# The key products of the two 16-head attentions moved to the end of a batch, three batches ahead

## The chip, the cores and the metric
The program runs on one core of one Trainium2 chip. The metric is the device time of one execution in microseconds (us); before the change the median of three runs is 4884.3 us (4883.45 to 4888.38).

## The reference, cut to what matters
The program is four layers of cross-attention and feed-forward over x (32 batches of 56 rows of 128) and a context (32 batches of 1500 rows of 128). The change touches the attention of layers L1 and L2, which have 16 heads of 8 columns:

```python
qh = split(q @ Wq.T + bq)          # (32, 16, 56, 8)
kh = split(k @ Wk.T + bk)          # (32, 16, 1500, 8), k is the context
vh = split(v @ Wv.T + bv)          # v is the context too
scores = jnp.einsum('bhqd,bhkd->bhqk', qh, kh) / jnp.sqrt(jnp.float32(D_K))
scores = jnp.where(mask[:, None, None, :] == 0, jnp.float32(-1000000000.0), scores)
attn = jax.nn.softmax(scores, axis=-1)
out = jnp.einsum('bhqk,bhkd->bhqd', attn, vh)
```

L1 has the mask and the biases, L2 has neither. Everything is float32.

## The kernel before, in words
`attention_16_heads` (L697) is called once for L1 and once for L2. All five instruction streams are unrolled over B = 32 batches. For one batch b they do the following.

- **Keys.** TensorE makes the keys of a batch as two items, ("keys", b, 0) with two products of 128x500 and ("keys", b, 1) with one (`keys_product`, L1020). VectorE empties them into the one tile `k_full` (L1189 with the mask of `valid` in L1, L1193 in L2), ScalarE copies them rounded into `k_hi` (L1131), GpSimd makes the remainder `k_lo` (L984). There is one `k_full`, one `k_hi` and one `k_lo`.
- **Moves.** SyncE (SP in the rows) issues 12 DMAs per batch in `move_keys` (L937 for `k_hi`, eight; L941 for `k_lo`, four), which lay the keys out by group of four heads in one of NKB = 3 tiles `keys`, on 96 partitions, so that one product carries high and low parts. In L1 two mask rows (L932) go with them. A tile is free when all scores of three batches earlier are made.
- **Rows.** Twelve items ("rows", b, n), n = 0 to 11, are the scores with the query on the partitions (`score_rows`, L1042); VectorE reduces them to maxima (L1202, L1205), and after n = 11 to one column `max_col` (L1211). ("turn", b, 0) transposes the column on TensorE (L1051), VectorE splits it (L1220, L1222), and SP moves it into two rows of the query tile (`move_maxima`, L949). The rows of batch b + 1 are made during batch b.
- **Scores and values.** In KT = 12 steps t, `scores(b, t, 0)` and `scores(b, t, 1)` (L1079) make a tile each, ScalarE takes the exponential (L1169) into `probs`, and `values(b, t)` (L1094, 16 small products) adds probabilities times values; the values are called in threes: 0 to 2 in step 4, 3 to 5 in step 7, 6 to 8 in step 10, and 9 to 11 at the start of the next batch. ScalarE then takes the sums (`take_acc`, L1154).

The order around the change is written out by hand, in lists that all engines follow in order. `before_scores` are the items at the start of a batch, `step_items[t]` those of step t; ("keys", 2, 0) in a list means the keys of two batches ahead. TensorE makes the first two items of `before_scores`, then values 9 to 11 of the batch before, then the other two, then the steps; in a step the first item comes between the two scores and the rest after them and after the values. The items share two pairs of PSUM banks in turn, so an item waits until the one two places before it is emptied. ScalarE goes through the same lists: after the two exponentials of a step it takes the keys or values of that step, and only then the next exponential. `prologue` is the order ahead of batch 0.

The first rows item of a batch (L1042, n = 0) waits for the queries, for all moves of that batch's keys, and in L1 for the mask rows. SP goes through one list too: in the turn for batch b it loads the context of b + 3 (`load_context`, L909, which waits for the last values product of b + 1, made in step 3 of batch b, because `ctx_T` has two tiles), then moves the keys of b + 2, then loads the mask row `valid` (L915) and the query terms (`load_terms`, L921) of b + 3, then moves the maxima of b + 1. GpSimd goes through the batches with `spread_queries(b)` (L994) ahead of `take_keys_lo(b, ·)`.

Of the kernel before, what the change touches and what calls it, by code (L numbers as in the profile page):

```python
# [20 lines left out]
B, SQ, D = 32, 56, 128  # L21
# [33 lines left out]
def bcast(ap, n, at):  # L55

    shape = list(ap.shape)
    return ap.unsqueeze(at).broadcast_to(shape[:at] + [n] + shape[at:])
# [638 lines left out]
def attention_16_heads(nc, s, a, layer, masked, biased):  # L697
# [14 lines left out]
    ROWS = PAIRS + SINGLES  # L712
# [1 line left out]

    before_scores = [("rows", 1, 0), ("keys", 2, 0), ("keys", 2, 1), ("rows", 1, 1)]
    step_items = [[("rows", 1, n)] for n in range(2, ROWS)] + [[], []]
    step_items[1].append(("values", 1, 0))
    step_items[3].append(("values", 1, 1))  # L720
    step_items[5].append(("sums", -1, 0))
    step_items[11].append(("turn", 1, 0))


    def of_batch(b, items):
        return [(kind, b + ahead, n) for kind, ahead, n in items if 0 <= b + ahead < B]

    prologue = [("keys", b, n) for b in range(2) for n in range(2)] + [("values", 0, n) for n in range(2)]
    prologue += [("rows", 0, n) for n in range(ROWS)] + [("turn", 0, 0)]
    scratch = list(prologue)  # L730
    for b in range(B):
        scratch += of_batch(b, before_scores)
# [29 lines left out]
    def key_cols(n):  # L762
        return slice(0, 2 * KC) if n == 0 else slice(2 * KC, SK)

    with ExitStack() as ctx:
        def sb(name, shape, dt=F32, on=ctx):
            return on.enter_context(nc.sbuf_tensor(f"{layer}a_{name}", shape, dt))
# [113 lines left out]
        keys = [sb(f"keys{n}", [KS, G, SK], F32R) for n in range(NKB)]  # L881
# [22 lines left out]
        @block.sync  # L904
        def _(sp):
            def load_context(b):
                if b >= 2:
                    sp.wait_ge(products, made[("values", b - 2, 1)])
                sp.dma_start(ctx_T[b % 2][:, :, :], a["ctx_T"][b].rearrange("d (t p) -> d t p", t=KT))\  # L909
                    .then_inc(ctx_loaded[b % 2], 16)  # L910

            def load_valid(b):
                if b:
                    sp.wait_ge(scratch_dve, by_dve[("keys", b - 1, 1)])
                sp.dma_start(valid[:, 0:SK], valid_dram[b:b + 1].broadcast_to([D, SK])).then_inc(valid_loaded, 16)  # L915

            def load_terms(b):
                if b >= 2:
                    sp.wait_ge(queries_made, (b - 1) * G)
                for k in range(3):  # L920
                    sp.dma_start(q_terms[b % 2][k * GR:(k + 1) * GR, :, :],  # L921
                                 q_dram[k, :, b * SQ:(b + 1) * SQ].rearrange("(g r) q -> r g q", g=G))\
                        .then_inc(terms_loaded[b % 2], 16)

            def move_keys(b):

                if b >= NKB:
                    sp.wait_ge(scores_made, (b - NKB + 1) * KT * 2)
                if b == 0:
                    sp.wait_ge(ones_set, NKB + NQ)  # L930
                if masked:
                    sp.dma_start(keys[b % NKB][KQ:KQ + 2, :, :].bitcast(F32), bcast(neg_dram[b], G, 1))\  # L932
                        .then_inc(neg_moved[b % NKB], 16)
                sp.wait_ge(k_hi_made, b * 2 + 2)
                for g in range(G):
                    for k in (0, 2):
                        sp.dma_start(keys[b % NKB][k * GR:(k + 1) * GR, g, :].bitcast(F32),  # L937
                                     k_hi[g * GR:(g + 1) * GR, :].bitcast(F32)).then_inc(keys_moved, 16)
                sp.wait_ge(k_lo_made, b * 2 + 2)
                for g in range(G):  # L940
                    sp.dma_start(keys[b % NKB][GR:2 * GR, g, :].bitcast(F32),  # L941
                                 k_lo[g * GR:(g + 1) * GR, :].bitcast(F32)).then_inc(keys_moved, 16)

            def move_maxima(b):
                sp.wait_ge(scratch_dve, by_dve[("turn", b, 0)])
                if b >= NQ:
                    sp.wait_ge(scores_made, (b - NQ + 1) * KT * 2)
                for k, part in enumerate((max_hi, max_lo)):
                    sp.dma_start(queries[b % NQ][SHIFT + k:SHIFT + k + 1, :, :].bitcast(F32), part[:, b % 2, :].bitcast(F32))\  # L949
                        .then_inc(row_moved, 16)  # L950

            if masked:
                load_valid(0)
            load_context(0)
            load_terms(0)
            load_terms(1)
            load_context(1)
            move_keys(0)
            if masked:
                load_valid(1)  # L960
            move_keys(1)
            if masked:
                load_valid(2)
            load_terms(2)
            load_context(2)
            move_maxima(0)
            for b in range(B):
                if b + 3 < B:
                    load_context(b + 3)
                if b + 2 < B:  # L970
                    move_keys(b + 2)
                if b + 3 < B:
                    if masked:
                        load_valid(b + 3)
                    load_terms(b + 3)
                if b + 1 < B:
                    move_maxima(b + 1)

        @block.gpsimd
        def _(pool):  # L980
            def take_keys_lo(b, n):
                cols = key_cols(n)
                pool.wait_ge(k_hi_made, b * 2 + n + 1)
                nc.gpsimd.tensor_tensor(k_lo[:, cols], k_full[:, cols], k_hi[:, cols].bitcast(F32), ALU.subtract)\  # L984
                    .then_inc(k_lo_made, 1)
                pool.wait_ge(k_lo_made, b * 2 + n + 1)

            def spread_queries(b):

                pool.wait_ge(terms_loaded[b % 2], 48 * (b // 2) + 48)  # L990
                if b >= NQ:
                    pool.wait_ge(scores_made, (b - NQ + 1) * KT * 2)
                for g in range(G):
                    nc.gpsimd.tensor_tensor(queries[b % NQ][0:KQ, g, :].rearrange("p (h q) -> p h q", h=HPG),  # L994
                                            bcast(q_terms[b % 2][:, g, :], HPG, 1),
                                            bcast(group_mask[0:KQ, :], SQ, 2), ALU.mult).then_inc(queries_made, 1)
                pool.wait_ge(queries_made, b * G + G)

            for n in range(NKB):
                nc.gpsimd.memset(keys[n][KQ:KS, :, :].bitcast(F32), 1.0).then_inc(ones_set, 1)  # L1000
            for n in range(NQ):
                nc.gpsimd.memset(queries[n][KQ:KS, :, :].bitcast(F32), 1.0).then_inc(ones_set, 1)
            pool.wait_ge(ones_set, NKB + NQ)
            for u in range(2):
                nc.gpsimd.memset(v[u][:, :, :, DK:DK + 1], 1.0).then_inc(ones_set, 1)
            pool.wait_ge(ones_set, NKB + NQ + 2)
            for b in range(B):
                spread_queries(b)
                for n in range(2):
                    take_keys_lo(b, n)  # L1010

        @block.tensor
        def _(pe):
# [46 lines left out]
            def make(item):  # L1060
                if item[0] == "keys":
                    keys_product(item)
                elif item[0] == "values":
                    values_product(item)
                elif item[0] == "rows":
                    score_rows(item)
                elif item[0] == "turn":
                    turn(item)
                else:
                    spread_sums(item)  # L1070
# [28 lines left out]
            for item in prologue:  # L1099
                make(item)  # L1100
            for b in range(B):
                for item in of_batch(b, before_scores[:2]):
                    make(item)
                if b:
                    for n in range(KT - GT, KT):
                        values(b - 1, n)
                for item in of_batch(b, before_scores[2:]):
                    make(item)
                for t in range(KT):
                    scores(b, t, 0)  # L1110
                    for item in of_batch(b, step_items[t][:1]):
                        make(item)
                    scores(b, t, 1)
                    if t > GT and (t - 1) % GT == 0:
                        for n in range(t - 1 - GT, t - 1):
                            values(b, n)
                    for item in of_batch(b, step_items[t][1:]):
                        make(item)
# [1135 lines left out]
```

## Time and profile before

| | us |
|---|---|
| runs, median of 3 | 4884.3 |
| profiled execution | 4889.31 |
| its span, first to last instruction | 4887.5 |
| first rows item of batch 2 to that of batch 30 ahead, L1 (28 periods) | 883.0 |
| the same in L2 (28 periods) | 860.7 |

The span is shared among the engines as PE 82%, DVE 55%, ACT 40%, POOL 20%. PE is TensorE (PEld its weight loads), DVE VectorE, ACT ScalarE, POOL GpSimd, SPq the queue from which SyncE issues DMAs. The attention of L1 fills the span from about 517 to 1582 us, that of L2 from about 1908 to 2945 us. PEclk in the windows is the granted clock of TensorE as a share of 2.4 GHz; 0.50 is 1.2 GHz. A row of the timeline gives start, duration, engine, source line, output and input, the count of instructions merged, and in brackets the idle time of the engine ahead of it and what ended it; "issue" says that the profile shows nothing that the engine waited for.

### The profile page before, as it was taken

The page shows a single profiled execution, that of the slowest core. Times are in us where ns is not written, and L with a number is a line of the kernel's source. Part 1 is how long each engine was busy: PE and PEld are TensorE (multiplying, and loading weights), DVE is VectorE, ACT ScalarE, POOL GpSimd, SP SyncE. Part 2 cuts the span into 40 slices and gives each one's busy share as a digit, 9 for nine tenths or more (in the row PEclk, how much of TensorE's full clock was granted, in tenths as well). Part 3 has the DMA queues.
Part 4 walks back from the last instruction along what each step waited for, and adds up shares of the span by engine and source line. Part 5 has one row for each costly group of instructions (what it writes and reads, how often), then busy time and mean ns, then how long its engine had stood idle before and what let it go on. Part 6 is the DMA issues. An engine that isn't in the chain of part 4 may idle for free. (4 is left out here: it accounts for less than half of the span.)

```text
span 4887.5 us, 95999 instructions
## 1 busy us (share of the span) xinstructions
PE 4009.1 (82%) x39918; PEld 2475.7 (51%) x39918; DVE 2668.6 (55%) x3910; ACT 1968.9 (40%) x3760; POOL 994.9 (20%) x979
## 2 busy tenths in 40 slices
PE   7799588888888896888888884358988988898888
PEld 4544366666666543566666662223444444444444
DVE  3233355555654332566656653337777777777751
ACT  3200144444444000344444452114555555555542
POOL 0000211111111002211111112102333343333330
PEclk8899699999999798899999997669999999999988
DMA  8700355555543001444444430000000000000000
GB/s 234 214 0 0 111 131 133 133 125 129 134 125 71 35 0 48 115 106 106 106 106 106 106 73 5 12 25 13 13 20 20 20 13 20 19 18 15 13 1 21
DMA packets 107980, 329.11 MB, mean 67 GB/s; under 512 B 54151, under 2 KB 55247, under 8 KB 107023
## 3 DMA queue, kind: packets, MB, share of 16 engines
q1 hardware_dynamic: 107567, 323.20, 25.4%
q8 instruction: 308, 5.05, 0.5%
q14 instruction: 105, 0.86, 0.1%
HBM read 168.20 MB, written 7.00 MB: 36 GB/s over the span
## 5 line engine op out<-in xcount | busy, mean ns | idle before, releaser
L1705 POOL TENSOR_TENSOR l_S<-l_S,l_shift 125x448 f32<-125x448 f32 (+1 forms) x416 | 459.3, 1138 | 311.2 <-ACT l_shift L1931 306.3
L1169 ACT ACTIVATE L2a_probs<-ps 125x448 f32<-125x448 f32 x768 | 375.0, 545 | 187.0 <-PE ps L1079 177.0
L1169 ACT ACTIVATE L1a_probs<-ps 125x448 f32<-125x448 f32 x768 | 374.9, 546 | 169.3 <-PE ps L1079 159.4
L1202 DVE TENSOR_REDUCE L1a_chunk_max<-ps 112x1 f32<-112x1000 f32 x256 | 300.5, 1196 | 249.2 <-PE ps L1042 248.7
L1759 PE MATMUL ps<-l_wk,l_xnT 128*125 128x512 f32 (+1 forms) x832 | 426.8, 639 | 2.3 <-ACT l_k_squares L1912 1.7
L1202 DVE TENSOR_REDUCE L2a_chunk_max<-ps 112x1 f32<-112x1000 f32 x256 | 300.6, 1196 | 218.1 <-PE ps L1042 217.7
L1777 PE MATMUL ps<-l_G,l_xnT 128*125 128x448 f32 (+1 forms) x832 | 388.8, 549 | 32.1 <-DVE l_S L2028 32.1
L1912 ACT ACTIVATE l_k_squares<-ps 125x512 f32<-125x512 f32 (+1 forms) x416 | 247.3, 595 | 413.5 <-PE ps L1759 413.5
L2008 DVE TENSOR_REDUCE l_norms<-l_k_squares 125x8 f32<-125x512 f32 (+1 forms) x416 | 278.7, 680 | 232.2 <-ACT l_k_squares L1912 230.2
L1042 PE MATMUL ps<-L1a_keys,L1a_queries 98*112 98x500 f32 x768 | 279.2, 446 | 142.1 <-issue 107.4
L1042 PE MATMUL ps<-L2a_keys,L2a_queries 96*112 96x500 f32 x768 | 279.2, 447 | 109.1 <-issue 73.0
L1809 PE MATMUL ps<-l_S,l_z 125*128 125x448 f32 x768 | 350.4, 547 | 0.0
L2028 DVE SCALAR_TENSOR_TENSOR l_S<-ps,l_neg_cols,l_inv_norms 125x448 f32<-125x448 f32 x384 | 261.4, 681 | 115.8 <-PE ps L1777 110.0
L1079 PE MATMUL ps<-L2a_queries,L2a_keys 98*125 98x224 f32 x1536 | 286.2, 290 | 6.3 <-ACT L2a_probs L1169 2.8
L1079 PE MATMUL ps<-L1a_queries,L1a_keys 100*125 100x224 f32 x1536 | 286.5, 290 | 2.3 <-ACT L1a_probs L1169 1.3
L1079 PEld LDWEIGHTS ps<-L2a_queries,L2a_keys 98*125 98x125 f32 x1536 | 243.0, 189 | 55.8 <-ACT L2a_probs L1169 9.3
L1079 PEld LDWEIGHTS ps<-L1a_queries,L1a_keys 100*125 100x125 f32 x1536 | 243.4, 189 | 51.4 <-ACT L1a_probs L1169 7.2
L1777 PEld LDWEIGHTS ps<-l_G,l_xnT 128*125 128x125 f32 (+1 forms) x832 | 143.6, 182 | 212.3 <-issue 132.5
L1759 PEld LDWEIGHTS ps<-l_wk,l_xnT 128*125 128x125 f32 (+1 forms) x832 | 143.6, 194 | 164.4 <-issue 97.7
L1935 ACT ACTIVATE l_S<-l_S 125x448 f32<-125x448 f32 (+1 forms) x416 | 222.4, 569 | 8.0 <-POOL l_S L1705 7.6
L1042 PEld LDWEIGHTS ps<-L1a_keys,L1a_queries 98*112 98x112 f32 x768 | 112.3, 182 | 195.8 <-issue 126.1
L994 POOL TENSOR_TENSOR L1a_queries<-L1a_q_terms,L1a_group_mask 96x224 fp32r<-96x224 f32 x128 | 67.4, 556 | 706.2 <-DMA L1a_q_terms<-L_q 706.1
(381 smaller groups left out, 6947.2 us busy)
## 6 DMA issues: line engine op xcount, KB each, us to landing
L1a_keys<-L1a_k_hi SPq DMA_DIRECT2D x256, 187.5 KB
L2a_keys<-L2a_k_hi SPq DMA_DIRECT2D x256, 187.5 KB
a_ctx_T<-in_ctx_T SPq DMA_DIRECT2D x32, 750.0 KB, 12.0
xn<-L_valid SPq DMA_DIRECT2D x32, 750.0 KB, 7.2
L1a_ctx_T<-in_ctx_T SPq DMA_DIRECT2D x32, 750.0 KB, 5.5
L1a_keys<-L1a_k_lo SPq DMA_DIRECT2D x128, 187.5 KB
L2a_ctx_T<-in_ctx_T SPq DMA_DIRECT2D x32, 750.0 KB, 5.9
L2a_keys<-L2a_k_lo SPq DMA_DIRECT2D x128, 187.5 KB
```

The costliest lines, as they stand in the source:

```text
L1042: mm = nc.tensor.matmul(s.ps[0:RW, bank(item) + half, 0:KC], queries[b % NQ][0:SHIFT, r // 2, r % 2 * RW:(r % 2 + 1) * RW], keys[b % NKB][ ...
L1079: mm = nc.tensor.matmul(s.ps[0:KP, i % 3, g % 2 * GC4:(g % 2 + 1) * GC4], keys[b % NKB][:, g, t * KP:(t + 1) * KP], queries[b % NQ][:, g, ...
L1169: nc.scalar.activation(probs[t % NPR][:, h * HQ // 2:(h + 1) * HQ // 2], s.ps[0:KP, i % 3, 0:HQ // 2], ACT.Exp).then_inc(probs_made, 1)
L1202: ins = nc.vector.tensor_reduce(chunk_max[:, n, 0:1], product, AX.XY, ALU.max)
L1705: nc.gpsimd.tensor_tensor(S[b % 2][0:r, t, :], S[b % 2][0:r, t, :], shift[0:r, :], ALU.add)\
L1759: nc.tensor.matmul(s.ps[0:rows(t), t % 2, 0:HID], xnT[b % 2][:, t * KP:t * KP + rows(t)], wk[:, :], start=True, stop=True).then_inc(k_made, 1)
L1777: nc.tensor.matmul(s.ps[0:rows(t), 2 + t % 2, 0:HQ3], xnT[b % 2][:, t * KP:t * KP + rows(t)], G[:, :], start=True, stop=True).then_inc(raw ...
L1809: mm = nc.tensor.matmul(s.ps[:, 6, 0:HQ3], z[b % 3][:, t, 1:D + 1], S[b % 2][:, t, :], start=(t == 0), stop=(t == KT - 1))
L1912: nc.scalar.activation(squares[0:rows(t), t % 2, :], s.ps[0:rows(t), t % 2, 0:HID], ACT.Square)\
L1935: nc.scalar.activation(S[b % 2][0:rows(t), t, :], S[b % 2][0:rows(t), t, :], ACT.Exp).then_inc(exps_made, 1)
L2008: nc.vector.tensor_reduce(norms[0:r, t, :], squares[0:r, t % 2, :].rearrange("p (h d) -> p h d", h=H8), AX.X, ALU.add).then_inc(reduced, 1)
L2028: ins = nc.vector.scalar_tensor_tensor(*heads_of, neg_cols[:, b, t:t + 1], factors, ALU.add, ALU.mult)
```

## The change
In the lists the keys leave the start of a batch. ("keys", 3, 0) stands in step 10 and ("keys", 3, 1) in step 11, three batches ahead in place of two; the turn moves from step 11 to step 10, ahead of the keys. On SP the keys of b + 2 are moved first and the context of b + 3 is loaded behind them. On GpSimd the remainder of the keys comes ahead of the queries. The prologue makes the values of batch 0 ahead of the keys of batch 1, and the keys of batch 2 at its end.

```diff
-    before_scores = [("rows", 1, 0), ("keys", 2, 0), ("keys", 2, 1), ("rows", 1, 1)]
+    before_scores = [("rows", 1, 0), ("rows", 1, 1)]
     step_items = [[("rows", 1, n)] for n in range(2, ROWS)] + [[], []]
     step_items[1].append(("values", 1, 0))
     step_items[3].append(("values", 1, 1))
     step_items[5].append(("sums", -1, 0))
-    step_items[11].append(("turn", 1, 0))
+    step_items[10] += [("turn", 1, 0), ("keys", 3, 0)]
+    step_items[11].append(("keys", 3, 1))
...
-    prologue = [("keys", b, n) for b in range(2) for n in range(2)] + [("values", 0, n) for n in range(2)]
-    prologue += [("rows", 0, n) for n in range(ROWS)] + [("turn", 0, 0)]
+    prologue = [("keys", 0, n) for n in range(2)] + [("values", 0, n) for n in range(2)]
+    prologue += [("keys", 1, n) for n in range(2)] + [("rows", 0, n) for n in range(ROWS)] + [("turn", 0, 0)]
+    prologue += [("keys", 2, n) for n in range(2)]
...
             for b in range(B):
-                if b + 3 < B:
-                    load_context(b + 3)
                 if b + 2 < B:
                     move_keys(b + 2)
                 if b + 3 < B:
+                    load_context(b + 3)
                     if masked:
                         load_valid(b + 3)
                     load_terms(b + 3)
...
             for b in range(B):
-                spread_queries(b)
                 for n in range(2):
                     take_keys_lo(b, n)
+                spread_queries(b)
...
-                for item in of_batch(b, before_scores[:2]):
+                for item in of_batch(b, before_scores[:1]):
                     make(item)
                 if b:
                     for n in range(KT - GT, KT):
                         values(b - 1, n)
-                for item in of_batch(b, before_scores[2:]):
+                for item in of_batch(b, before_scores[1:]):
                     make(item)
```

## Rows read from the trace of the kernel before
**Rows 1.** Waits of the engines, 626 to 1540 us (L1): total, times, longest.
```profile
PE ps L1042 <- issue: 107.4, 29, 5.8
...
PE ps L1094 <- issue: 6.3, 10, 1.6
...
PE ps L1042 <- DVE L1a_k_full L1189: 4.8, 29, 0.2
```
**Rows 2.** The same, 2010 to 2900 us (L2).
```profile
PE ps L1042 <- issue: 73.0, 27, 4.4
...
PE ps L1094 <- issue: 18.2, 20, 1.5
```
**Rows 3.** Windows: stretch, length, busy time of each engine, PEclk, DMA share, GB/s.
```profile
626.05:1509.03 882.98, 739.90 (x13692) 567.40 (x13693) 514.84 (x532) 418.87 (x812) 159.44 (x168) 0.93 0.51 129
2010.45:2871.17 860.72, 735.82 (x13693) 561.25 (x13693) 514.80 (x532) 418.80 (x812) 159.21 (x168) 0.94 0.44 105
1003.64:1018.68 15.04, 14.61 (x156) 10.10 (x156) 8.92 (x8) 6.43 (x12) 5.70 (x6) 0.85 0.02 5
1018.68:1035.90 17.22, 11.97 (x335) 10.06 (x334) 9.47 (x11) 8.52 (x17) 0.00 (x0) 0.99 0.93 228
```
**Rows 4.** Timeline of one batch of L1, 1003 to 1036 us.
```profile
1003.64 1.17 PE L1042 MATMUL ps<-L1a_keys,L1a_queries 98*112 98x500 f32 x2 [5.33 <-issue]
...
1010.78 0.38 PE L1079 MATMUL ps<-L1a_queries,L1a_keys 100*125 100x224 f32 x2
...
1019.42 6.71 SPq L937 DMA_DIRECT2D L1a_keys<-L1a_k_hi  x8
...
1026.17 3.11 SPq L941 DMA_DIRECT2D L1a_keys<-L1a_k_lo  x4
...
1027.24 2.97 ACT L1169 ACTIVATE L1a_probs<-ps 125x448 f32<-125x448 f32 x6 [1.17 <-PE ps L1079]
...
1027.82 0.29 PEld L1042 LDWEIGHTS ps<-L1a_keys,L1a_queries 98*112 98x112 f32 x2
...
1028.38 1.04 PE L1079 MATMUL ps<-L1a_queries,L1a_keys 100*125 100x224 f32 x6
...
1030.03 0.17 DVE L1211 TENSOR_REDUCE L1a_max_col<-L1a_chunk_max 112x8 f32<-112x16 f32 x1
...
1035.90 1.15 PE L1042 MATMUL ps<-L1a_keys,L1a_queries 98*112 98x500 f32 x2 [4.46 <-issue]
```
**Rows 5.** Timeline of the start of one batch of L2, 2685 to 2691 us.
```profile
2685.65 0.68 PE L1042 MATMUL ps<-L2a_keys,L2a_queries 96*112 96x500 f32 x2 [2.12 <-issue]
2686.16 1.84 PE L1020 MATMUL ps<-L2a_ctx_T,L2a_wk 128*128 128x500 f32 x4
...
2687.93 1.37 PE L1094 MATMUL ps<-L2a_probs,L2a_v 125*9 125x56 f32 x96
2688.04 1.26 DVE L1193 TENSOR_SCALAR L2a_k_full<-ps,L2a_bias_k 128x1000 f32<-128x1000 f32 x1 [0.41 <-PE ps L1020]
...
2689.34 1.04 ACT L1131 ACTIVATE L2a_k_hi<-L2a_k_full 128x1000 fp32r<-128x1000 f32 x1 [5.12 <-DVE L2a_k_full L1193]
...
2690.63 0.38 PE L1079 MATMUL ps<-L2a_queries,L2a_keys 98*125 98x224 f32 x2
```
**Rows 6.** Timeline of L1, end of batch 29 and start of batch 30.
```profile
1533.25 0.62 PE L1042 MATMUL ps<-L1a_keys,L1a_queries 98*112 98x500 f32 x2
...
1536.60 0.61 PE L1042 MATMUL ps<-L1a_keys,L1a_queries 98*112 98x500 f32 x2
```
**Rows 7.** Timeline of PE in L1, step 10 of one batch.
```profile
1130.67 1.04 PE L1094 MATMUL ps<-L1a_probs,L1a_v 125*9 125x56 f32 x45 [1.56 <-issue]
```
**Rows 8.** Windows of one microsecond around gaps in the values of step 10, columns as above.
```profile
1131.00:1132.00 1.00, 1.00 (x36) 0.82 (x24) 0.00 (x0) 0.00 (x0) 0.00 (x0) 0.50 1.13 186
2373.00:2374.00 1.00, 1.00 (x17) 0.81 (x9) 0.00 (x0) 0.34 (x1) 0.00 (x0) 1.00 1.01 234
```
**Rows 9.** Timeline of PE in L2, step 10 of the batch at 2349 us.
```profile
2372.85 0.37 PE L1094 MATMUL ps<-L2a_probs,L2a_v 125*9 125x56 f32 x12 [1.54 <-issue]
```

## The prediction
> **What bounds the kernel now.** I read the waits first. In both 16-head layers TensorE's largest stop is one per batch, ahead of the first rows item (L1042, n = 0): 107.4 us over 29 batches in L1, 3.7 each, and 73.0 over 27 in L2, 2.7 each [rows 1, 2]. "Issue" names no releaser, so the code has to: this item waits for the twelve key moves, whose landing the view does not link. The windows support that. In a batch of L1 the DMA engines are 0.02 busy for the first 15.0 us and 0.93 busy, at 228 GB/s, for the other 17.2 [rows 3], up to the moment when TensorE restarts. The timeline says why so late: the moves are issued from 1019.42, behind a context load that waits for step 3, the last four until 1029.28, and the rows item starts at 1035.90, 6.6 us later [rows 4]. So the transfers of a batch are squeezed into its second half and TensorE waits for their end.
>
> The gap costs a second time. After it the clock is at 1.2 GHz: over the 28 periods PEclk is 0.93 in L1 and 0.94 in L2 [rows 3]. One batch of L2 starts without the drop and takes 2690.63 - 2685.65 = 4.98 us to its first scores [rows 5]; a cold one takes 1010.78 - 1003.64 = 7.14 [rows 4]. A drop thus costs about 2.2 there; I use 2.0 for one elsewhere.
>
> The periods are 882.98/28 = 31.53 us in L1 and 860.72/28 = 30.74 in L2 [rows 3].
>
> **The period without gap or drop.** 4.98 for the warm start [rows 5], 1027.82 - 1010.78 = 17.04 from the first scores to rows item 11 [rows 4], 1536.60 - 1533.25 = 3.35 from there to the next batch where no move was waited for [rows 6]: 25.4 us.
>
> **What the change adds to it.** Let rows item 11 start at 0 (1027.82).
> - *The turn one step earlier.* Today three pairs of scores follow item 11, from 1028.38, about 0.32 each [rows 4]. The turn now stands ahead of the third, which started near 1029.03. It needs `max_col`, ready at 1030.03 + 0.17 = 1030.20 [rows 4], and about 0.15 of hand-over (estimate). TensorE stands from 1.2 to 2.5: **1.3 us added**. Behind the turn in TensorE's queue are a score, values 6 to 8, the keys, everything.
> - *The keys themselves.* The same three products, warm: 1.77 for the pair (2687.93 - 2686.16); 0.85 for the single one, which is 4.98 less 0.51 and 0.55 for the rows, 1.77, and 1.3 for the values [rows 5]. They are already in the 25.4.
> - *ScalarE in order.* After the turn come a score (0.35), the values (1.3), the key pair: it ends at 2.5 + 0.35 + 1.3 + 1.77 = 5.9. VectorE starts to empty 0.11 later and takes 1.26, ScalarE follows in 0.03 and takes 1.04 [rows 5]: `k_hi` is done at 8.4. Only then come the two exponentials of step 11, 0.49 each (2.97/6 [rows 4]), until 9.4. TensorE does scores, single key, scores and rows by 7.9 and values 9 and 10 by 8.8; values 11 wait: **0.65 added**. `k_hi` of the second half and `take_acc` end near 10.2, ahead of the exponential that the next first scores ask for.
> - *Relieved:* VectorE starts the batch without a key backlog. The wait for `k_full` (4.8/29 = 0.17 [rows 1]) goes, and as much again behind it, by estimate: **0.3 saved**.
> - *Banks.* Item two places earlier: the first key item needs item 11 emptied, which it is; the next rows item needs the key pair emptied, at 5.9 + 0.11 + 1.26 = 7.3, and comes at 7.4. Nothing.
> - *GpSimd:* the remainder now runs at 8.4 to 12.1, the queries behind it, both a full batch ahead of use. Nothing.
> - *SP.* The same 12 key issues, now ahead of context, `valid` and terms. With a new batch starting at 7.4, the tile is free at once and `k_hi` complete at 10.0, that is 2.6 us into the batch; the eight issues take 6.7, the four 3.1 [rows 4]: done at 12.4 (was 25.6). Landing 6.6 later is 19, against a use at 27: 8 us of cover, and the gap goes. Context and `valid` are next; by the 17.2 us of all a batch's transfers they are in by about 2.6 + 17.2 = 20 [rows 3]. The keys ask for the context at 24 and for `valid` at 26. If that cover went, each late microsecond would cost one per batch. The maxima are moved one step earlier and gain cover.
>
> The Trainium skill (DMA: Bandwidth & Descriptors, "Two DMAs through the same engine are not ordered") says that on one engine's queue descriptors start in the order of issue. By that rule the context cannot overtake the key moves and the order on SP counts. The trace has the context always in front and cannot show it; my 20 us assumes it.
>
> New period: 25.4 + 1.3 + 0.65 - 0.3 = **27.1 us**.
>
> **Instruction gaps.** TensorE also stops inside runs of values (a semaphore cannot do that in the middle of a step's sixteen products): 6.3/28 = 0.22 a period in L1, 18.2/28 = 0.65 in L2 [rows 1, 2]. They fall in stretches where the DMA engines are full. The full stretch moves, it does not shrink: I leave them as they are.
>
> **New clock drops.** The two added stops are short, but such stops can drop the clock: one of 1.56 us in the values of step 10 did (0.50 in the next slice), one of 1.54 did not (1.00) [rows 7 to 9]. I take a drop in 3 periods of 10: 0.3 x 58 x 2.0 = 35 us. The Trainium skill (TensorE: Matmul & The Clock Gate, "Why this matters for your kernels") allows longer gaps between bursts than these. By it there would be no drop and the time 35 us lower, 4677; the 1.56 us row disagrees, so I keep the 35.
>
> **The sum.** L1 saves 31.53 - 0.22 - 27.1 = 4.2 a period, L2 30.74 - 0.65 - 27.1 = 3.0. The gap stands at 29 batch starts of each layer: 29 x 7.2 = 209. Less 35 for the clock, less 5 for the turn's stop in the last two batches, which had no gap to lose (4 x 1.3), plus 3 for the start of the two layers, where rows no longer wait for both batches' keys (estimate, 0 to 8). 209 - 35 - 5 + 3 = 172. The profiled execution of 4889.3 (span 4887.5, 1.8 around it) would be 4717; it lay 5 above the median of the runs, so from 4884.3 I predict **4712 us**.
>
> **The rivals.**
> - *The clock falls in every batch.* The stops of 1.3 and 0.65 lie 6 us apart, and 1.56 alone has sufficed once. Price 58 x 2.0 = 116 in place of 35: 4793. For it: the drop after 1.56 [rows 7, 8]. Against: the products between the stops are dense, and 1.54 did nothing [rows 8, 9].
> - *The stops are absorbed.* No drop (-35), ScalarE's 0.65 hidden (58 x 0.65 = 38), and the standing of the turn lets the instruction supply catch up in L2 (0.5 x 29 = 15): 4624.
> - *Context or `valid` late.* If transfers beside busy engines take 9 us longer than the 17.2, the keys of L1 wait some 4 us in step 10: 29 x 4 = 116, 4828. Against: 228 GB/s was measured with the engines working.
> - *Slower: the gap is not the moves but TensorE's instructions*, held up behind full DMA queues. Then the stop only goes where the queues are now full, the middle of the batch, and the added stops remain: 58 x (1.3 + 0.65 - 0.3) = 96, 4980. For it: the releaser is unnamed and small gaps of this kind exist. Against: the largest inside the values is 1.6 [rows 1], those ahead of the rows item reach 5.8 and always stand at the one instruction that waits for the moves. It decides if more than 3.6 us a period (the mean saving before the clock) come back in the middle.
> - *The change does not do what it says:* the moves could start early only if the tile is free at the batch's start. It is, by its own wait (scores of the batch before), the same moment.
>
> **Chances.** Forecast 0.62 (own range 4665 to 4765), clock in every batch 0.15, absorbed 0.12, late transfers 0.06, instruction supply 0.05. The range 4620 to 4800 takes in the first three and leaves out the other two. A measurement of this kernel tells about 0.2%, 10 us. Faster 0.94, same 0.01, slower 0.05.
>
> **What would show it.** Right: the unnamed wait of L1042 falls from 107 and 73 us to a few; the DMA engines are full from some 3 us into a batch and idle at its end; a wait of the turn for `max_col` near 1.3 appears, and one of the values for the exponentials near 0.65; periods near 27 to 28. Wrong: a wait of L1020 or of VectorE's key emptying for the context or `valid`; unnamed gaps over 2 us in the middle of a batch; PEclk still near 0.93.

## The result and the profile after

The changed kernel takes 4668.3 us (median of 4 runs, 4666.1 to 4670.8) against 4883.9 for the kernel before on the same chip: a ratio of 0.9562, 95% interval 0.9545 to 0.9579. It is faster by 4.4%. The forecast was 4712 us, the range 4620 to 4800.

From L717 on the changed kernel's lines stand one lower than before: rows L1043, scores L1080, values L1095, key products L1021, turn L1052. In the experiments they shift again, by up to ten lines (rows are L1041, L1044 or L1052, values L1093, L1096, L1102 or L1104); the tile names stay the same.

First the waits of TensorE in the changed kernel over 28 periods of L1 (621.79 to 1393.36 us, from one `take_acc` to another), then over 28 of L2 (1891.01 to 2658.65): total, times, longest.

```profile
PE ps L1052 <- DVE L1a_max_col L1212: 38.3, 28, 1.4
PE ps L1043 <- DVE L1a_chunk_max L1203: 18.6, 56, 0.5
PE ps L1095 <- ACT L1a_probs L1170: 6.9, 27, 0.3
PE ps L1043 <- DVE L1a_k_full L1190: 4.6, 27, 0.2
PE ps L1095 <- issue: 2.1, 1, 2.1
...
PE ps L1052 <- DVE L2a_max_col L1212: 38.3, 28, 1.4
...
PE ps L1095 <- ACT L2a_probs L1170: 7.2, 28, 0.3
```

The unnamed wait of the rows item, 107.4 and 73.0 us before [rows 1, 2], is not there at all, and no wait for the context or the mask row has come in its place. The turn's wait for `max_col` is new, 1.37 us in every batch. The unnamed gaps in the values, 6.3 and 18.2 us before, are one gap of 2.1.

The windows of the same stretches and of one batch, whose first rows item starts at 730.36 and whose `take_acc` at 732.85 (length, busy time of each engine, PEclk, DMA share, GB/s):

```profile
621.79:1393.36 771.57, 684.40 (x13693) 540.88 (x13694) 514.82 (x532) 427.01 (x812) 159.44 (x169) 1.00 0.55 147
1891.01:2658.65 767.64, 682.56 (x13693) 540.18 (x13694) 514.78 (x532) 426.98 (x813) 159.29 (x169) 1.00 0.48 118
...
736.00:740.00 4.00, 3.92 (x29) 3.44 (x30) 2.32 (x3) 2.28 (x5) 1.59 (x4) 1.00 0.97 228
744.00:748.00 4.00, 3.20 (x43) 2.54 (x45) 3.84 (x4) 2.49 (x6) 0.00 (x0) 1.00 0.97 352
752.00:756.00 4.00, 3.38 (x104) 2.39 (x104) 0.96 (x4) 0.59 (x2) 0.00 (x0) 1.00 0.03 6
```

Against [rows 3]: 28 periods take 771.6 and 767.6 us where they took 883.0 and 860.7, which is 27.56 and 27.42 a period for 31.53 and 30.74. PEclk is 1.00 where it was 0.93 and 0.94. The DMA engines are full in the first half of a batch and idle in its last steps: the transfers have been turned round. 3.97 + 3.32 us over 29 batches are 211 us of the 218.5 by which the profiled execution fell (4889.3 to 4670.8).

That batch in the timeline of the changed kernel, its start and its end:

```profile
730.36 0.69 PE L1043 MATMUL ps<-L1a_keys,L1a_queries 98*112 98x500 f32 x2 [0.17 <-DVE L1a_k_full L1190]
732.04 0.62 ACT L1132 ACTIVATE L1a_k_hi<-L1a_k_full 128x500 fp32r<-128x500 f32 x1
732.20 0.58 PE L1095 MATMUL ps<-L1a_probs,L1a_v 125*9 125x56 f32 x32 [0.25 <-ACT L1a_probs L1170]
732.69 5.86 SPq L939 DMA_DIRECT2D L1a_keys<-L1a_k_hi  x8
738.59 3.37 SPq L943 DMA_DIRECT2D L1a_keys<-L1a_k_lo  x4
742.00 0.59 SPq L911 DMA_DIRECT2D L1a_ctx_T<-in_ctx_T  x1
...
750.20 0.62 PE L1043 MATMUL ps<-L1a_keys,L1a_queries 98*112 98x500 f32 x2
750.66 0.60 PE L1080 MATMUL ps<-L1a_queries,L1a_keys 100*125 100x224 f32 x4
752.30 0.17 DVE L1212 TENSOR_REDUCE L1a_max_col<-L1a_chunk_max 112x8 f32<-112x16 f32 x1
752.62 0.26 PE L1052 MATMUL ps<-ident,L1a_max_col 112*8 112x112 f32 x1 [1.37 <-DVE L1a_max_col L1212]
...
754.33 1.94 PE L1021 MATMUL ps<-L1a_ctx_T,L1a_wk 128*128 128x500 f32 x4
756.31 1.91 DVE L1190 SCALAR_TENSOR_TENSOR L1a_k_full<-ps,L1a_bias_k,xn 128x1000 f32<-128x1000 f32 x2 [2.84 <-PE ps L1021]
```

The moves start 0.03 us after ScalarE has finished the second half of `k_hi` (732.66), and are all issued at 741.96. Counted from the batch's first rows item, as in [rows 4], that is 2.3 to 11.6 us into it; before they were issued 15.8 to 25.6 us into it. The turn stands from 751.25 to 752.62, and behind it the key pair.

### The profile page after: what moved, and what is told of

It is laid out like the page before. It is cut to its first block and busy times, and to the rows that moved or that the text cites. A ratio compares the mean times of both kernels' runs of the same rounds, so it can differ in the third digit from the quotient of the medians.

```text
span 4668.8 us, 95999 instructions
## 1 busy us (share of the span) xinstructions
PE 3896.2 (83%) x39918; PEld 2422.1 (52%) x39918; DVE 2668.5 (57%) x3910; ACT 1986.2 (43%) x3760; POOL 995.1 (21%) x979
## 3 DMA queue, kind: packets, MB, share of 16 engines
q8 instruction: 308, 5.05, 0.5%
## 5 line engine op out<-in xcount | busy, mean ns | idle before, releaser
L1170 ACT ACTIVATE L1a_probs<-ps 125x448 f32<-125x448 f32 x768 | 383.2, 544 | 192.0 <-PE ps L1080 178.3
L1170 ACT ACTIVATE L2a_probs<-ps 125x448 f32<-125x448 f32 x768 | 383.4, 544 | 191.1 <-PE ps L1080 177.5
L1043 PE MATMUL ps<-L1a_keys,L1a_queries 98*112 98x500 f32 x768 | 261.8, 423 | 56.3 <-DVE L1a_k_full L1190 22.8
L1080 PE MATMUL ps<-L1a_queries,L1a_keys 100*125 100x224 f32 x1536 | 308.0, 300 | 0.5 <-ACT L1a_probs L1170 0.4
L1080 PE MATMUL ps<-L2a_queries,L2a_keys 98*125 98x224 f32 x1536 | 306.9, 299 | 0.9 <-issue 0.5
L1043 PE MATMUL ps<-L2a_keys,L2a_queries 96*112 96x500 f32 x768 | 262.1, 424 | 53.1 <-DVE L2a_chunk_max L1203 21.4
L1080 PEld LDWEIGHTS ps<-L1a_queries,L1a_keys 100*125 100x125 f32 x1536 | 247.0, 188 | 70.3 <-issue 27.8
L1080 PEld LDWEIGHTS ps<-L2a_queries,L2a_keys 98*125 98x125 f32 x1536 | 246.3, 187 | 70.0 <-issue 27.6
L985 POOL TENSOR_TENSOR L1a_k_lo<-L1a_k_full,L1a_k_hi 128x1000 fp32r<-128x1000 f32 x64 | 114.6, 1791 | 659.3 <-ACT L1a_k_hi L1132 656.7
L985 POOL TENSOR_TENSOR L2a_k_lo<-L2a_k_full,L2a_k_hi 128x1000 fp32r<-128x1000 f32 x64 | 114.5, 1789 | 649.3 <-ACT L2a_k_hi L1132 646.7
```

The lines of the kernel that those rows point to most:

```text
L1043: mm = nc.tensor.matmul(s.ps[0:RW, bank(item) + half, 0:KC], queries[b % NQ][0:SHIFT, r // 2, r % 2 * RW:(r % 2 + 1) * RW], keys[b % NKB][ ...
L1080: mm = nc.tensor.matmul(s.ps[0:KP, i % 3, g % 2 * GC4:(g % 2 + 1) * GC4], keys[b % NKB][:, g, t * KP:(t + 1) * KP], queries[b % NQ][:, g, ...
L1170: nc.scalar.activation(probs[t % NPR][:, h * HQ // 2:(h + 1) * HQ // 2], s.ps[0:KP, i % 3, 0:HQ // 2], ACT.Exp).then_inc(probs_made, 1)
```

## The experiments

| kernel | median, us | ratio | 95% interval |
|---|---|---|---|
| the change | 4668.3 | 0.9562 | 0.9545 to 0.9579 |
| turn_late | 4607.0 | 0.9444 | 0.9420 to 0.9468 |
| keys_step9 | 4563.7 | 0.9357 | 0.9333 to 0.9380 |
| context_first | 4840.8 | 0.9910 | 0.9886 to 0.9934 |
| sp_order_only | 4573.9 | 0.9383 | 0.9355 to 0.9411 |
| pool_old_order | 4667.3 | 0.9571 | 0.9555 to 0.9587 |
| extra_traffic | 4873.7 | 0.9987 | 0.9971 to 1.0003 |
| copies_early | 4827.2 | 0.9891 | 0.9863 to 0.9918 |
| copies_late | 4701.6 | 0.9646 | 0.9630 to 0.9662 |
| sp_order_turn10 | 4650.1 | 0.9534 | 0.9518 to 0.9550 |

Differences below are of these medians; taken from the ratios, which leave the chip out, they come out within 8 us of them.

**The turn back in step 11** (turn_late), the keys staying in steps 10 and 11:

```diff
-    step_items[10] += [("turn", 1, 0), ("keys", 3, 0)]
-    step_items[11].append(("keys", 3, 1))
+    step_items[10].append(("keys", 3, 0))
+    step_items[11] += [("turn", 1, 0), ("keys", 3, 1)]
...
-                    for item in of_batch(b, step_items[t][:1]):
+                    for item in of_batch(b, step_items[t][:t != 10]):
...
-                    for item in of_batch(b, step_items[t][1:]):
+                    for item in of_batch(b, step_items[t][t != 10:]):
```

> The changed kernel with the turn back in step 11 (the keys stay in steps 10 and 11, the second half now behind the last scores of step 11). Theory A (the gap at a batch's start was the landing of the key moves; the turn's early place costs its whole wait, 38.3 us over 28 periods = 1.37 each): the wait of L1052 for max_col goes, the period of 27.36 us becomes about 26.0 and the time 4668 - 58 x 1.3 = 4593 us. Rival (the turn's wait only fills time that ScalarE needs anyway, so the wait moves to the values): time within 10 us of 4668.

It took 4607.0, 61 us less than the change. The turn's wait is gone and a smaller one of the single key product is new:

```profile
PE ps L1021 <- DVE L1a_k_full L1190: 22.0, 27, 0.8
```

The waits are read over 661 to 1538 us. So the stop at the turn is a cost of the change and of its own place, worth about 61 us.

**The key pair in step 9, the turn alone in step 10** (keys_step9):

```diff
-    step_items[10] += [("turn", 1, 0), ("keys", 3, 0)]
+    step_items[9].append(("keys", 3, 0))
+    step_items[10].append(("turn", 1, 0))
     step_items[11].append(("keys", 3, 1))
```

> The changed kernel with the first key item in step 9, behind rows item 11 and the scores, the turn alone in step 10, the second key item in step 11. Theory A: the key pair (1.7 us) fills the turn's wait of 1.37, and k_hi is ready before the exponentials of step 11, so the wait of values 11 (about 0.4) goes too: period 25.6, time 4668 - 58 x 1.75 = 4566 us. Rival (ScalarE, which now stands for k_full between the exponentials of steps 9 and 10, becomes late for the last values): period about 27, time about 4650.

4563.7 us, the lowest of all, though only 10 us below sp_order_only, whose interval it overlaps; the period falls to 715.98/28 = 25.57 us. The key pair now fills the time in which VectorE makes `max_col`: the turn's wait is all but off the list (2.7 us in two stops), and what is left are short waits for banks. The window of 28 periods of L1, and waits over 661 to 1538 us:

```profile
625.32:1341.30 715.98, 673.12 (x13693) 536.44 (x13693) 514.84 (x532) 424.50 (x812) 159.93 (x169) 1.00 0.59 158
...
PE ps L1044 <- DVE L1a_chunk_max L1204: 19.0, 57, 0.5
PE ps L1022 <- DVE L1a_chunk_max L1207: 7.6, 27, 0.3
```

**SP's old order under the moved keys** (context_first): in the changed kernel SP again loads the context of b + 3 ahead of the moves.

```diff
             for b in range(B):
+                if b + 3 < B:
+                    load_context(b + 3)
                 if b + 2 < B:
                     move_keys(b + 2)
                 if b + 3 < B:
-                    load_context(b + 3)
                     if masked:
```

> The changed kernel with SP's old order: the context of b + 3 ahead of the key moves of b + 2, so that the moves wait for step 3 again. Theory A: the moves start about 10.5 us into the batch instead of 2.6; with 17.2 us of transfers in L1 they end at about 27.7 against a period of 27.4, so a gap of 0.5 to 1.5 us returns in L1 with a clock drop in many batches, less in L2: 4668 + 20 to 120, say 4720 us. Theory C (what mattered was that the key products left the batch's start, the order on SP is secondary): 4668 within 10. Theory B (TensorE waited for instructions while the DMA engines are full at a batch's end): unnamed gaps in the values of steps 7 and 10 return, 0.2 to 0.7 a period, 4690 to 4710, without a wait at the rows item.

A miss: 4840.8. The waits over L1 and then L2, and the two windows:

```profile
DVE L1a_k_full L1191 <- DMA xn<-L_valid: 165.0, 26, 7.4
PE ps L1044 <- DVE L1a_k_full L1191: 91.2, 27, 4.7
...
PE ps L1096 <- issue: 19.8, 18, 2.3
...
661.50:1538.70 877.20, 712.42 (x13204) 568.64 (x13204) 498.07 (x513) 411.79 (x783) 153.60 (x163) 0.91 0.50 125
2037.10:2845.10 808.00, 704.83 (x13693) 554.02 (x13694) 515.14 (x532) 427.56 (x812) 159.37 (x169) 0.97 0.46 112
```

L2 has a mean period of 28.9 and no unnamed wait at the rows item: there the keys made early do remove the gap without SP's new order. 16 of its 28 periods are within 0.2 us of the 27.36 of the changed kernel; the others are longer, by unnamed gaps in the values (L1096, the third line) and by clock drops in 8 of them. L1 has the mask row `valid`, which SP issues behind the moves. Keys made in step 10 want it about 4 us earlier than keys made behind the first rows item (754.33 against some 758.2 in the batch shown above); it is late, and VectorE (6.3 us a batch) and TensorE (3.4) stand for it. Moving the keys forward needs the new SP order in L1, not for the moves but for the load behind them.

**SP's new order alone** (sp_order_only): the kernel before with nothing of the change but this.

```diff
             for b in range(B):
-                if b + 3 < B:
-                    load_context(b + 3)
                 if b + 2 < B:
                     move_keys(b + 2)
                 if b + 3 < B:
+                    load_context(b + 3)
                     if masked:
```

> The kernel before with SP's new order alone: the key moves of b + 2 ahead of the context of b + 3, all else as before (keys made at the batch's start). Theory A: the moves start when k_hi is ready, about 8.5 us into the batch instead of 15.8, and land near 25; the gap of 3.7 and 2.7 us and the cold start (2.2) go, no stop of the turn is added: period 25.5 to 26.5 us, time 4884 - 58 x 5 = 4594 us, if the context, which lands last now, is in time for the next batch's start; if it is late by 1 to 3 us a period, 4650 to 4770. Theory C (the key products at the batch's start are what costs): within 20 us of 4884. Theory B: 4860 or more, since the DMA engines are still full at the batch's end.

4573.9, that is 94 us below the whole change. Windows of L1 and L2, and one batch of L1 with its first rows item, the end of its `k_hi` and the start of its moves (its `take_acc` is at 746.77):

```profile
615.11:1349.20 734.09, 688.65 (x13693) 539.64 (x13693) 514.86 (x533) 418.62 (x814) 159.41 (x169) 1.00 0.59 155
1843.90:2564.00 720.10, 684.15 (x13694) 538.36 (x13693) 514.83 (x533) 418.61 (x813) 159.23 (x169) 1.00 0.52 126
...
740.50 0.61 PE L1041 MATMUL ps<-L1a_keys,L1a_queries 98*112 98x500 f32 x2
...
746.24 0.62 ACT L1130 ACTIVATE L1a_k_hi<-L1a_k_full 128x500 fp32r<-128x500 f32 x1 [0.78 <-DVE L1a_k_full L1188]
...
746.89 6.22 SPq L937 DMA_DIRECT2D L1a_keys<-L1a_k_hi  x8
```

The keys of b + 2 are still made at the batch's start here, and `k_hi` is complete at 746.86, 6.4 us behind the first rows item. The moves follow 0.03 us later. In the kernel before, `k_hi` was complete at 1011.92 and the moves started at 1019.42, so 7.5 us of their delay were the context load ahead of them and its wait for step 3. Taking these 7.5 us away is enough to close the gap; that the whole change starts the moves another 4 us earlier (2.3 us into the batch against 6.4) buys nothing more at the rows item. The whole gain is in this reordering.

In L1 the mean period is 26.22, 0.5 above L2. Part of that is 8.8 us in 16 unnamed gaps in the values; L2 has none.

**The turn alone on top of it** (sp_order_turn10):

```diff
-    step_items[11].append(("turn", 1, 0))
+    step_items[10].append(("turn", 1, 0))
```

> The kernel before with SP's new order, and of the rest of the change only the turn, moved from step 11 to step 10. It prices the turn alone from the other side. Theory: the stop of 1.37 us for max_col comes back in all 60 or so batches and nothing hides it: 4573.9 + 61 (what putting the turn back gave the changed kernel) = 4635 us, up to 4573.9 + 58 x 1.37 = 4653; the other 33 us of what the whole change lies above the SP order alone belong to the keys in steps 10 and 11. Rival: the turn costs little without the keys behind it (they delay ScalarE together): under 4610, and the cost is the pair's.

4650.1, the theory's upper end; the wait is again there, 38.2 us in 28 batches of L1 and 38.3 in L2. With turn_late this makes a square. The period that is met most often, in L1:

| | keys at the start | keys in steps 10, 11 |
|---|---|---|
| turn in step 11 | 25.72 | 26.31 |
| turn in step 10 | 26.72 | 27.36 |

The turn costs 1.00 or 1.05, the keys 0.59 or 0.64: within 0.05 us neither depends on the other. The windows of sp_order_turn10 in L1 and L2 show something more:

```profile
624.42:1376.48 752.06, 679.56 (x13693) 541.58 (x13692) 514.72 (x533) 421.71 (x814) 159.34 (x169) 1.00 0.57 151
1873.77:2638.83 765.06, 692.71 (x13693) 553.90 (x13692) 514.66 (x533) 421.55 (x813) 159.18 (x169) 0.98 0.49 118
...
1892.27:1894.27 2.00, 2.00 (x78) 1.89 (x81) 0.52 (x2) 0.54 (x1) 0.00 (x0) 0.63 0.03 8
1920.54:1922.54 2.00, 2.00 (x101) 1.79 (x102) 0.53 (x2) 0.54 (x1) 0.00 (x0) 1.00 0.04 12
```

In L2, 11 of 28 periods are 28.2 to 28.3 instead of 26.72: after the same stop of 1.37 us the clock falls in some batches (first of the two lines behind the turn) and not in others (second). One such drop costs 1.5 us.

**GpSimd's old order** (pool_old_order):

```diff
             for b in range(B):
+                spread_queries(b)
                 for n in range(2):
                     take_keys_lo(b, n)
-                spread_queries(b)
```

> The changed kernel with GpSimd's old order: the queries of a batch ahead of the remainder of its keys. The queries of b + 3 wait for the last scores of b, so the remainder, ready about 1.3 us after that in the changed kernel's order (3.65 us of work begun before the batch ends), would be ready near 7 us into the batch. SP issues the remainder's moves behind the eight k_hi moves, 8 us into the batch. Expected: no change, 4668 within 10 us. Rival (the moves of the remainder slip by some us and with them the context and the mask row, which the keys of step 10 wait for in L1): 4690 to 4720, with a wait of VectorE for the mask row.

4667.3: this part of the change is worth nothing, as was said.

**Extra traffic** (extra_traffic): with three further copies of 0.75 MB per batch in the device memory.

```diff
                     take_keys_lo(b, n)
                 spread_queries(b)
+                if b:
+                    pool.wait_ge(extra_loaded, 48 * b)
+                for k in range(3):
+                    nc.gpsimd.dma_start(extra[k], a["ctx_T"][b]).then_inc(extra_loaded, 16)
+            pool.wait_ge(extra_loaded, 48 * B)
```

> The changed kernel with 2.25 MB more traffic a batch (three copies of the context from DRAM to DRAM, issued by GpSimd behind the queries, about 5 us into a batch; nobody waits for them but GpSimd a batch later). Then the DMA engines are full through steps 7 to 11, as before the change, while no key move has to wait for step 3. Theory B' (the unnamed gaps in the values are instruction supply held up by full DMA engines, and they bring clock drops): the gaps come back at 0.2 to 0.7 us a period and PEclk falls below 1.00 in L2: 4668 + 40 to 100 us. Rival (the gaps depended on the old place of the keys or on the old turn): in L2 no gaps, period 27.4 as without the traffic. In L1 the mask row may also be late, up to 3 us a period, 80 us more under either.

4873.7, as slow as before. The unnamed gaps of theory B' are back, and the clock falls too (0.96 in L1, 0.95 in L2), but their size was missed: 205 us over the change, where the gaps and drops were priced at 40 to 100. The wait for the mask row, which was to add up to 80, is 6.1 us in L1. The waits of TensorE over 661 to 1538 us, and the window of L1:

```profile
PE ps L1102 <- issue: 44.2, 36, 2.5
...
638.60:1490.60 852.00, 717.51 (x13693) 558.50 (x13694) 515.53 (x532) 427.11 (x812) 201.56 (x253) 0.96 0.71 209
```

**Two copies, early or late.** To see what brings these gaps, the same copies (two of them) were sent after step 0 of a batch, and in a second run after step 9, with `+ 10` in place of the `+ 1`:

```diff
+                if b >= 2:
+                    if b > 2:
+                        pool.wait_ge(extra_loaded, 32 * (b - 2))
+                    pool.wait_ge(scores_made, ((b - 2) * KT + 1) * 2)
+                    for k in range(2):
+                        nc.gpsimd.dma_start(extra[k], a["ctx_T"][b]).then_inc(extra_loaded, 16)
+            pool.wait_ge(extra_loaded, 32 * (B - 2))
```

> The changed kernel, plus two copies per batch of the context within the device memory (1.5 MB) on GpSimd's queue, sent after step 0 of each batch; their output is used by nothing. From the run with three copies (5.7 us more DMA work per batch by share times length, 0.71 x 30.43 - 0.55 x 27.56 = 6.4) two should be about 4.3 us. What is open: why TensorE's unnamed gaps vanished with the change although the DMA engines are full as long as before, and came back with three copies. Theory P (place): the gaps arise only when the full stretch lies beside steps 10, 11 and the start of a batch. Here the full stretch grows from 0.5-16.5 us to about 0.5-21 us into a batch and ends in front of step 10, so there are few gaps: 4668 to 4690 us, PE's unnamed waits under 10 us per layer. Rival Q (length or amount of a batch's traffic): gaps as with three copies, two thirds of their price: 4668 + 137 = about 4800 us, in this run and in the next alike.

> The same two copies per batch, sent when step 9 of the batch is done, so that they lie beside steps 10, 11 and the start of the next batch, where the changed kernel has the DMA engines idle. Theory P (place): the unnamed gaps are back in the values (L1095 of the changed kernel), about 1 us per period by the 44.2 and 36.0 us of the run with three copies less the part that was step 7 to 9, and a clock drop of 2.0 us in about three periods of ten: 58 x 1.6 = 93, 4760 us (4710 to 4800). Rival Q (amount): the same time as with the early copies, whatever that is. A third, N: neither place nor amount alone, but the context and key moves being delayed past their use; then late copies cost next to nothing, 4670, and early ones show a wait of the rows or of the keys' emptying.

All three theories fall. Early took 4827.2 (+159), late 4701.6 (+33), the reverse of the place theory, and not alike as the amount theory had it. Nor are context and moves late (theory N): the named waits of TensorE are no longer than in the changed kernel, and the late copies do cost something. The early copies in L1: waits over 661 to 1480, then one batch with its `take_acc` at 743.71.

```profile
PE ps L1104 <- issue: 39.5, 33, 2.5
...
761.53 0.55 PE L1104 MATMUL ps<-L1a_probs,L1a_v 125*9 125x56 f32 x14 [1.75 <-issue]
...
743.71:752.00 8.29, 7.83 (x53) 6.66 (x54) 5.81 (x5) 5.37 (x11) 5.25 (x8) 1.00 0.93 234
758.00:762.00 4.00, 2.25 (x100) 1.75 (x98) 2.28 (x3) 0.70 (x2) 0.00 (x0) 0.95 1.01 241
762.00:766.00 4.00, 4.00 (x17) 3.40 (x14) 1.90 (x2) 1.83 (x4) 0.00 (x0) 0.50 0.68 255
```

The engines are full, or nearly, from the start of the batch through to 762 and beyond. At 759.8 TensorE stops inside values 3 to 5 for 1.75 us, and then the clock is at 1.2 GHz (0.50). By their place in the period 30 of the 33 gaps lie 15.1 to 16.2 us (values 3 to 5) or 20.7 to 23.9 us (values 6 to 8) behind `take_acc`. Those are the runs densest in instructions, in the tail of the lengthened full stretch. In the changed kernel that stretch ends 15 to 16 us behind `take_acc` (between 748 and 749 in the batch shown), within values 3 to 5 and well ahead of values 6 to 8, which fits that they are spared. The late copies make a second, shorter full stretch and have 11 gaps of together 8.3 us in L1.

The trace shows what TensorE waits for in these gaps. The page of the changed kernel lists the fetches of instructions as DMA traffic of their own, and one of their packets lies just ahead of the gap at 759.78 to 761.53 (second line, from 758.5 to 761.53 in copies_early):

```profile
q8 instruction: 308, 5.05, 0.5%
...
q8 instruction: 1, 0.02, 2.8%
```

They are 5.05 MB in 308 packets, 16.4 KB each. The packet of that gap lands at 760.07, and TensorE goes on 1.46 us later. It is so each time. All 33 gaps of L1 end 1.2 to 1.7 us behind the landing of such a packet, and so do the 11 of the late copies, the 16 of sp_order_only, the one of the changed kernel and the 30 in the values of the kernel before. With 103 landings in the 819 us, a moment picked at random would have one at that distance in some 6% of cases. Block for block, over 28 periods of L1, those of copies_early that have a gap behind them land a median of 35 products further on in TensorE's program than the same blocks of the changed kernel, and the rest at the same place (median 0). So the gaps are late instructions, and the extra traffic is what made them late. How full engines hold a block up is open: its packet takes about 1 us in either kernel. The same mark tells this kind of stop from the gap at the rows item: of its 56 stops before [rows 1, 2], 5 end at that distance, and chance alone gives 3 or 4.

The Trainium skill (Runtime: NRT & Kernel Launch, "Instruction fetch mechanics") says that a sequencer refills its instructions in blocks of 16 KiB through a DMA queue of its own, and calls the cost mostly hidden. The size agrees; hidden it is not while the engines are full.

## Why the prediction was right

- **The gap at the rows item** was the landing of moves issued late. Shown: with the moves issued as soon as `k_hi` is complete, by either kernel with SP's new order, it is gone from both layers. The rival that TensorE's instructions make this gap is out: in sp_order_only, which moves the transfers alone, no such stop comes back where the engines are full now, and the 56 stops before lack the mark of a late block.
- **The period without gap or drop, 25.4:** 25.72 in sp_order_only, 0.3 more. The waits for `k_full` were in the rows that it was added up from and explain nothing of that. 0.11 is a slip of the sum: 1027.82 is the start of a weight load, the product of rows item 11 starts at 1027.93. The other 0.24 is the start of a batch, 4.98 in [rows 5] and 5.22 in sp_order_only (first rows item at 1889.12, first scores at 1894.34): the batch of [rows 5] stood behind a stop of 2.12 us.
- **The turn, +1.3:** the wait is 1.37, and from rows item 11 to the next first rows item the way does grow by 1.30 (3.36 us in sp_order_only, 4.66 in sp_order_turn10). The period grows by 1.0 only, since the same start of a batch, now behind a stop, is 0.3 shorter (4.93 for 5.22).
- **ScalarE in order, +0.65:** keys in steps 10 and 11 cost 0.59 to 0.64, so the size was right. The wait that was to show it is only 0.26 (6.9/27). In the batch shown values 9 to 11 take 1.74 us (730.98 to 732.72) where such a run takes 1.30 elsewhere, so 0.44 is found at that place. The rest is not traced, and with the turn in step 11 the keys cost as much by another wait (`k_full`, 0.8). That the size came out is in part luck.
- **Relieved, -0.3:** did not come. The wait for `k_full` is 4.8 us before [rows 1] and 4.6 after; it has moved from one rows item to another, and the waits for banks emptied into `chunk_max` are 18.6 us in 56, where they were 13.8 in 29.
- The sum of these was 27.1; the period met in nearly all batches is 27.36. Over 58 batches that is 15 us too little.
- **Instruction gaps left as they are, 0.22 and 0.65 a period:** mis-sized. 29 x 0.87 = 25 us were kept; 2.1 were found. The stretch in which the engines are full was rightly said to move and not to shrink, but it moved away from the values that suffer.
- **Clock drops, 35 us:** mis-sized. Only two of 56 turn stops and the one gap of 2.06 us were followed by a drop, 28.97 us in place of 27.36 for each of the two: some 5 us in all. The share of 3 in 10 is what sp_order_turn10 shows in L2 (11 of 28), so the risk was real, and nothing here says why the changed kernel is mostly free of it. The longer gaps that the Trainium skill allows (TensorE: Matmul & The Clock Gate, "Why this matters for your kernels") would have given 4677, nearer to the time, yet the drops after 1.37 us speak against the rule.
- **SP, GpSimd:** as worked out. The moves wait for `k_hi` until 2.3 us into the batch (2.6 forecast) and are all issued at 11.6 (12.4), the engines are full until about 18 of the 20 allowed, and context and mask row are in time. GpSimd nothing, shown. That SP's order counts is shown by context_first in L1 and by sp_order_only.

The two over-sized costs (30 + 23 us) less the 15 are 38 of the 44 us by which 4668 lies under 4712; the rest is in the starts and ends of the layers and within the spread. The forecast came this near partly because errors of either sign offset each other.

What the prediction did not see is that its gain and its costs come from different lines. Of its parts only SP's order pays (4879.6 on that chip to 4573.9, -306 us, alone); the turn and the keys, which it priced nearly right, take 94 back.

## What to carry to other kernels

When an unnamed wait stands where a transfer lands, look first at what is queued ahead of that transfer's issue: here one load with a late wait stood before moves that were ready, and swapping them was worth more than the whole rewrite around it. Split a change into its lines and price each, since one can pay for the others. When work is moved to an engine's in-order queue, put it where a short wait already stands: the key pair ahead of the turn cost nothing, the key items behind it 0.6 us a batch and the bare turn 1.0.

## What was not expected of the hardware

- With the DMA engines full, TensorE runs short of instructions in its densest runs: 0.2 to 2.5 us each, 33 gaps in some 27 periods of L1 with two copies sent early, one in the changed kernel, each ending 1.2 to 1.7 us behind the landing of a block of instructions. Where in a full stretch they begin is open: in the kernel before they came in shorter full stretches too.
- The same stop of 1.37 us was followed by a fall to 1.2 GHz in 11 of 28 batches of L2 in one kernel and in 1 of 28 in another; a drop cost 1.5 us.
- Traffic alone, with TensorE's named waits as they were, cost 159 us (two copies per batch, early) or 33 us (late).
